# A graph network layer with routed experts: expert weights loaded in four chained parts, the input added under the last attention head, register reads moved

## The reference, cut to what matters

```python
x = x + relu(agg + res)                    # L0_gnn: 12 heads of 64, relu over all 768 columns
z = layernorm(x)
top = argmax(z @ Wg + bg)                  # L0_ffn: one of 4 experts for each node
h = gelu(z @ W1[top] + b1[top])            # 768 -> 384
x = x + h @ W2[top] + b2[top]              # 384 -> 768
# L1_gnn: dinv = rsqrt(degree), used from here on
```

## Time and profile before

| | us |
|---|---|
| median of 3 runs (lowest, highest) | 1097.67 (1097.63, 1098.87) |
| profiled execution, its time | 1098.94 |
| profiled execution, its span | 1097.2 |
| PE busy | 992.9 (90%) |
| DVE busy | 611.1 (56%) |
| ACT busy | 288.5 (26%) |
| POOL busy | 60.2 (5%) |

### The profile page before, as it was taken

How to read it: one execution, slowest core, us unless ns; L and a number is a source line. 1 busy time by engine, 2 the same in 40 slices (tenths; PEclk the granted TensorE clock), 3 DMA queues, 4 the chain that set the end, 5 groups by cost and what they waited for, 6 DMA issues and landing times. The chain is left out here.

```text
span 1097.2 us, 15664 instructions
## 1 busy us (share of the span) xinstructions
PE 992.9 (90%) x5694; PEld 801.6 (73%) x5694; DVE 611.1 (56%) x1273; ACT 288.5 (26%) x780; POOL 60.2 (5%) x114
## 2 busy tenths in 40 slices
PE   5999998999999999948099993999999999999996
PEld 4777675999999999935056662566998557878784
DVE  7787796999999999967223222753211112232331
ACT  1434342355444555113011100122111012200100
POOL 2000000000000000011112210100000000000000
PEclk9999999899999999969589997899999999999999
DMA  3100000000000000347412224324200001200001
GB/s 118 33 1 1 24 29 1 23 25 24 23 23 34 34 23 32 130 136 273 182 44 87 87 80 176 128 76 159 88 1 1 1 0 56 86 29 29 21 15 51
DMA packets 23912, 65.26 MB, mean 59 GB/s; under 512 B 4104, under 2 KB 7956, under 8 KB 23728
## 3 DMA queue, kind: packets, MB, share of 16 engines
q1 hardware_dynamic: 21408, 54.20, 13.6%
q0 software_dynamic: 2080, 10.23, 2.8%
q10 hardware_dynamic: 368, 0.07, 0.0%
HBM read 47.74 MB, written 16.76 MB: 59 GB/s over the span
## 5 line engine op out<-in xcount | busy, mean ns | idle before, releaser
L754 PE MATMUL O<-X,masks 125*125 125x264 f32 x1200 | 280.9, 333 | 2.8 <-DVE masks L891 2.8
L751 PE MATMUL O<-X,CSR 125*125 125x132 f32 x1080 | 245.6, 227 | 0.0
L754 PEld LDWEIGHTS O<-X,masks 125*125 125x125 f32 x1200 | 222.9, 188 | 3.0 <-issue 3.0
L891 DVE SCALAR_TENSOR_TENSOR masks<-a2b,NA,CSR 125x375 fp32r<-125x375 f32 (+1 forms) x360 | 212.9, 645 | 17.4 <-PEq L738 9.6
L751 PEld LDWEIGHTS O<-X,CSR 125*125 125x125 f32 x1080 | 205.6, 190 | 0.0
L389 PE MATMUL pc<-ohs_a,ohd 125*125 125x512 f16 (+1 forms) x399 | 84.1, 352 | 0.0
L1572 PE MATMUL pw<-W 128*125 128x384 f32 x240 | 81.5, 497 | 1.0 <-ACT W L1708 1.0
L1792 DVE SCALAR_TENSOR_TENSOR UL<-pw,dinv,UH 125x768 fp32r<-125x768 f32 x20 | 20.4, 1018 | 110.9 <-ACT UH L1715 110.9
L1572 PE MATMUL pw<-region,xr_or_h 128*125 128x384 f32 x240 | 77.6, 486 | 0.0
L581 DVE TENSOR_SCALAR ohs_a<-iota,srcf 125x1250 f16<-125x1250 f16 x132 | 71.4, 541 | 0.0
L578 DVE TENSOR_SCALAR ohd<-iota,dstf 125x125 f16<-125x125 f16 x220 | 53.8, 251 | 28.5 <-PE pc L389 25.3
(11 more groups left out here) (225 smaller groups left out, 1388.9 us busy)
## 6 DMA issues: line engine op xcount, KB each, us to landing
a2b<-a_rows SPq DMA_DIRECT2D x12, 610.4 KB
W<-in_L_ffn_W SPq DMA_DIRECT2D x1, 4608.0 KB, 15.9
WM<-in_L_ffn_W SPq DMA_DIRECT2D x1, 4608.0 KB, 27.6
xr_or_h<-in_x SPq DMA_DIRECT2D x10, 375.0 KB
region<-in_x SPq DMA_DIRECT2D x2, 1875.0 KB
z_rows<-region SPq DMA_DIRECT2D x10, 375.0 KB
region<-y_rows SPq DMA_DIRECT2D x10, 375.0 KB
x_rows<-xr_or_h SPq DMA_DIRECT2D x10, 375.0 KB
```

The lines of the kernel that those rows point to most:

```text
L751: nc.tensor.matmul(O[0:P, bank, d - d0, 2 * DP:4 * DP], CSR[:, s, d * P:(d + 1) * P], X[:, buf, s, 4:6, :].rearrange("p k d -> p (k d)"), ...
L754: ins = nc.tensor.matmul(O[0:P, bank, d - d0, 0:4 * DP], kept, X[:, buf, s, 0:4, :].rearrange("p k d -> p (k d)"), start=s == 0, stop=s == ...
L891: nc.vector.scalar_tensor_tensor(masks[:, s, 0:(d1 - d0) * P], a2b[:, buf, d0 * P:d1 * P], NA1[:, s, bass.ds(h, 1)], CSR[:, s, d0 * P:d1 * ...
```

## The change

Expert weights are loaded by expert, in four parts. The first is issued where all weights were; the second after the fifth store of z, once the first has landed; the third and fourth in the experts block, once the first three gathers have landed and each after the part before it. One semaphore counts them, and the first layer on PE waits for the part of its expert by the value in the register. The relu and the sum with the second copy of x leave `prepare`: eleven heads' columns are summed before `combine(H - 1)`, the last head's after it, each in two operations over five tiles. POOL answers two inverse roots, then makes constants, with two more answers between them; `gdeg` is asked and answered last, and `dinv` is made after `slot_out`. The turn of `b1` on PE and its copy on ACT go behind the tiles. PE reads its last two registers, and DVE its last nine, in the experts block. The slow path gets the same sum (it is not taken here).

```diff
--- before.py
+++ after.py
@@ -880,6 +880,14 @@
             def _(dve):
                 chains = [chain(dve, "dve_chain2"), chain(dve, "dve_chain2_slow")]
 
+                def add_x(k, heads):
+
+                    for n in range(2):
+                        h = slice(n * NT // 2, (n + 1) * NT // 2)
+                        c = slice(heads[0] * DH, heads[1] * DH)
+                        dve.wait_ge(s_xi[n], 16)
+                        k.mark(nc.vector.scalar_tensor_tensor(XR[:, h, c], XR[:, h, c], 0.0, XI[:, h, c], ALU.max, ALU.add))
...
                     head(H - 1, 1, last=True)
+                    k.wait()
+                    add_x(k, (0, H - 1))
                     for step in combine(H - 1):
                         pass
+                    k.wait()
+                    add_x(k, (H - 1, H))
+                    k.wait()
 
...
-        s_wm1, s_wm2, s_b4 = sem("moe_w1_in"), sem("moe_w2_in"), sem("moe_biases_in")
+        s_wm, s_b4 = sem("expert_weights_in"), sem("moe_biases_in")
+
+        def load_expert(sp, e):
+            sp.dma_start(WM1[:, e], a["L0_ffn_W1"][e].rearrange("(k p) h -> p k h", p=128)).then_inc(s_wm, 16)
+            sp.dma_start(WM2[:, e], a["L0_ffn_W2"][e].rearrange("(m p) d -> p m d", p=128)).then_inc(s_wm, 16)
+
...
-                    sp.dma_start(WM1, a["L0_ffn_W1"].rearrange("e (k p) h -> p e k h", p=128)).then_inc(s_wm1, 16)
-                    sp.dma_start(WM2, a["L0_ffn_W2"].rearrange("e (m p) d -> p e m d", p=128)).then_inc(s_wm2, 16)
+                    load_expert(sp, 0)
                     for t in range(NT):
                         sp.wait_ge(s_z3, t + 1)
                         sp.dma_start(z_t[:, t, :], ZA[:, t, :]).then_inc(s_zst, 16)
+                        if t == NT // 2 - 1:
+                            sp.wait_ge(s_wm, 32)
+                            load_expert(sp, 1)
                     sp.wait_ge(s_gt3, NT)
...
-                    answer_inverse_sqrt(pool, gdeg[:, :])
+                    answer_inverse_sqrt(pool, rstd[:, 0:1])
+                    answer_inverse_sqrt(pool, rstd[:, 1:2])
                     nc.gpsimd.memset(ones16[:, :], 1.0).then_inc(s_c3, 1)
                     nc.gpsimd.memset(minus1, -1.0).then_inc(s_c3, 1)
                     pool.wait_ge(s_c3, 2)
                     nc.gpsimd.affine_select(out=notabove[:, :], in_=minus1, compare_op=ALU.is_ge, fill=0.0,
                                             base=0, pattern=[[-1, P]], channel_multiplier=1).then_inc(s_c3, 1)
+                    answer_inverse_sqrt(pool, rstd[:, 2:3])
                     nc.gpsimd.iota(slot_i[:, :], [[1, 128]], base=-ST, channel_multiplier=0).then_inc(s_c3, 1)
                     nc.gpsimd.iota(tile_i[:, :], [[ST, 16]], base=0, channel_multiplier=0).then_inc(s_c3, 1)
                     nc.gpsimd.iota(node_i[:, :], [[P, NT]], base=1, channel_multiplier=1).then_inc(s_c3, 1)
+                    answer_inverse_sqrt(pool, rstd[:, 3:4])
                     nc.gpsimd.iota(spare_i[:, :], [[ST, 16]], base=N + 1, channel_multiplier=1).then_inc(s_c3, 1)
                     nc.gpsimd.memset(inner[:, :, 1:NT], 1.0)
                     nc.gpsimd.memset(inner[:, :, 0:1], 0.0).then_inc(s_c3, 1)
                     for e in range(NEXP):
                         ins = nc.gpsimd.memset(order[:, e:e + 1], float(NEXP - e))
                     ins.then_inc(s_c3, 1)
-                    for t in range(NT):
+                    for t in range(4, NT):
                         answer_inverse_sqrt(pool, rstd[:, t:t + 1])
+                    answer_inverse_sqrt(pool, gdeg[:, :])
                     pool.wait_ge(s_zst, 16 * (NT + 1))
...
-                    pe.wait_ge(s_b1, 16)
-                    nc.tensor.transpose(pb1[:, 0:NEXP * MH], b1r[:, :], ident[0:NEXP * MH, 0:NEXP * MH]).then_inc(s_b1t, 1)
+                    turn_z(0)
                     pe.wait_ge(s_wg, 32)
-                    turn_z(0)
...
                     turn_gates(NT - 1)
+                    pe.wait_ge(s_b1, 16)
+                    nc.tensor.transpose(pb1[:, 0:NEXP * MH], b1r[:, :], ident[0:NEXP * MH, 0:NEXP * MH]).then_inc(s_b1t, 1)
                     pe.wait_ge(s_oh3, 1)
...
-                    for j in range(NS):
+                    for j in range(NS - 2):
...
-                    act.wait_ge(s_b1t, 1)
-                    nc.scalar.copy(b1T[:, :, :].rearrange("p e m -> p (e m)"), pb1[:, 0:NEXP * MH])
...
-                    ch(nc.vector.tensor_scalar(gdeg[:, :], deg[:, :], 1.0, None, ALU.max),
-                       nc.vector.tensor_scalar(seen[:, :], deg[:, :], 0.0, None, ALU.is_gt))
-                    degrees = ask_inverse_sqrt(dve)
-
                     def prepare(t):
 
-                        if t % (NT // 2) == 0:
-                            dve.wait_ge(s_xi[2 * t // NT], 16)
-                        nc.vector.scalar_tensor_tensor(XR[:, t, :], XR[:, t, :], 0.0, XI[:, t, :], ALU.max,
-                                                       ALU.add).then_inc(s_x1, 1)
-                        dve.wait_ge(s_x1, t + 1)
...
+                    ch(nc.vector.tensor_scalar(gdeg[:, :], deg[:, :], 1.0, None, ALU.max),
+                       nc.vector.tensor_scalar(seen[:, :], deg[:, :], 0.0, None, ALU.is_gt))
+                    degrees = ask_inverse_sqrt(dve)
...
-                       nc.vector.memset(start[:, 0:1], 0.0),
-                       nc.vector.tensor_tensor(dinv[:, :], gdeg[:, :], seen[:, :], ALU.mult))
+                       nc.vector.memset(start[:, 0:1], 0.0))
...
-                    for j in range(NS):
+                    dve.wait_ge(s_ra, degrees)
+                    ch(nc.vector.tensor_tensor(dinv[:, :], gdeg[:, :], seen[:, :], ALU.mult))
+                    for j in range(NS - 9):
                         experts_dve.append(expert_of(dve, j))
...
+                    for j in range(SLOTS):
+                        sp.wait_ge(s_xs[j], 16)
+                    for e in range(2, NEXP):
+                        sp.wait_ge(s_wm, 32 * e)
+                        load_expert(sp, e)
                     sp.wait_ge(s_h, NS)
...
+                        pe.wait_ge(s_wm, experts[j] * 32 + 32)
...
                     turn_slots(0)
-                    pe.wait_ge(s_wm1, 16)
+                    for j in range(NS - 2, NS):
+                        experts_pe.append(expert_of(pe, j))
                     first_layer(0)
                     turn_slots(1)
-                    pe.wait_ge(s_wm2, 16)
...
                     copy_slots(0)
+                    for j in range(NS - 9, NS):
+                        experts_dve.append(expert_of(dve, j))
                     copy_hidden(0)
```

More of the change, by code:

```diff
@@ L1016, in slowly @@
                         k.end(H)
+                    k.wait()
+                    add_x(k, (0, H))
+                    k.wait()
                 either(dve, quickly, slowly)
@@ L1096, in program @@
             s_wg, s_b1, s_b1t, s_c3 = sem("gate_w_in"), sem("moe_b1_in"), sem("moe_b1_turned"), sem("constants3")
-            s_x1, s_z3, s_zt3 = sem("x1_done"), sem("z3_ready"), sem("z3_transposed")
+            s_z3, s_zt3 = sem("z3_ready"), sem("z3_transposed")
             s_ztc3, s_g3 = sem("z3t_copied"), sem("gates_done")
@@ L1216, in _ @@
                     copy_gates(NT - 1)
+                    act.wait_ge(s_b1t, 1)
+                    nc.scalar.copy(b1T[:, :, :].rearrange("p e m -> p (e m)"), pb1[:, 0:NEXP * MH])
                     act.wait_ge(s_eid, 1)
```

## The result

| | us |
|---|---|
| before, median of 4 runs (lowest, highest) | 1097.65 (1095.82, 1098.87) |
| changed kernel, median of 4 runs (lowest, highest) | 1087.38 (1086.01, 1087.85) |
| ratio, 95% interval | 0.9906 [0.9889, 0.9923] |
| changed kernel, profiled execution and its span | 1086.93, 1085.2 |

The change takes 10.3 us off; the forecast was 11.2 (1086.5). The page of the changed kernel (PE's busy tenths and its granted clock, 40 slices of 27.1 us) shows where: the three slices that read 4, 8, 0 in the earlier trace rows read 5, 9, 1.

The account below looks back on a forecast made before the run. The last store of z, delayed by weight loads on its five DMA engines, was taken to bound the gating block. -12.3 + 0.95 + 0.05 + 0.1 = -11.2 us, from 1097.67 to 1086.5, range 1085.0 to 1088.4 (chance 0.75).

Parts of the forecast that it names:

- What bounds the kernel: Gating block: PE waits for the first gather, which the last store of z releases; the slot map isn't the bound.
- Two parts fewer, -12.3: Gating block: two weight parts fewer ahead of the last store, 6.15 us each, bring it 12.3 us earlier.
- Block opens 0.95 later: Start of gating block: the last head's two operations and the waits delay all engines, +0.95 us.
- The sum under the last head, +0.05: Attention's end: two sums with x take 7.66 us in DVE's idle 7.64, costing +0.05 us.
- Compute chain: Gating block: first z near 484, L1265 at 512.8, map at 521.5, seven before the stores; no gain counted.
- Waits by expert and reads: Experts block: per-slot weight waits cost +0.1 us, up to 2 if exposed; moved register reads cost 0.
- Last store to first transpose, "plus 7.7": Barrier after gating: first transpose follows the last store's landing by 7.7 us, POOL's drain lying between.
- stores pass part 1: Rival, gating block: part 1 doesn't delay the last five stores, which end 6.15 us earlier; 1080.4 us, chance 0.04.
- What would show it: Signs in the trace: first z near 484, DMA share 0.32 with one bump, gather at 528 to 529, transpose 536.
- Gaps at the pieces: Rival, gating block: five DMA engines stand still around each part, stores end 4.6 us later; 1091.1 us, chance 0.09.
- a low clock in gating: Rival, gating block: PE's clock stays low, map at 531.9, later than the stores; 1089.8 us, chance 0.04.
- a dear register wait: Rival, `first_layer`: the register wait drains PE's sequencer, a cold start in each of 13 slots; 1103.7 us, chance 0.03.

Follow-up runs that it names:

- e4: Changed kernel with each store of z cut into 120 and 5 rows: 1081.03 us.
- e8: Kernel before, all weights still ahead of the stores, with each store of z cut into 120 and 5 rows: 1086.88 us.
- e2: Changed kernel with all expert weights loaded ahead of the stores as before, the rest of the change kept: 1098.34 us.
- e6: Changed kernel with a third weight part (part 2) also issued between the fifth and sixth store of z: 1093.05 us.
- e1: Kernel before with only the four weight parts, their chain and the wait by expert added: 1087.68 us.
- e7: Changed kernel with all thirteen register reads of PE and of DVE back in the gating block: 1085.85 us.
- e3: Changed kernel with part 1 of the weights issued behind the tenth store of z instead of the fifth: 1086.46 us.
- e5: Changed kernel with only the first gather in the gating block, the next two at the start of the experts block: 1084.43 us.
- e11: Changed kernel with z stores and y loads cut into 120 and 5 rows, one gather and four PE and ACT reads before the barrier: 1075.46 us.

## Why the prediction was right, point by point

**What bounds the kernel: right.** The gather waits for the last store in the changed kernel as in the earlier trace rows, with the map at 521.66, seven before it. e4 and e8 confirm it from the other side: with the stores out of the way the map releases the gather.

**Two parts fewer, -12.3: right in kind, 0.8 too much.** e2 against the changed kernel gives 11.5, e6 6.0 for one part; I had used 6.15 from the earlier trace rows, half the distance of two landings.

**Block opens 0.95 later: too little, it is 1.6 at SP's first issue.** From zero to SP's first issue are 480.20 - 479.09 = 1.11 us before and 480.73 - 478.05 = 2.68 after. The two operations take 0.89, near the forecast: two of 0.49 are 0.98, which leaves nothing of my 0.95 for the waits that it was to cover as well. What is missing is the wait that follows them: in the kernel before, DVE's sequencer is at its drain at 479.7, while L915 still runs; in the changed one the operations end at 479.80 and the drain starts at 480.4. At the gather e2 shows 1.3, so 0.3 more than forecast.

**The sum under the last head, +0.05: right.** Two operations from 466.56 take 7.55 in all (forecast 7.66), and L907 is then released by ACT's `ev` after 0.17 of idle time, where the earlier trace rows had 7.64. From the end of the last mask to the zero it is 11.40 us before and after.

**Compute chain: right.** L1285 (L1265 before) starts at 513.00 (forecast 512.8), `slot_out` at 521.66 (521.5), and first z is stored from 483.94 (484). With all weights ahead of the stores it gives nothing, as e2 shows. With two parts fewer it gives next to nothing either: the map alone would allow the gather at 521.66 + 0.80, 6.2 us before the stores do, and even e1's old chain is about even with its stores.

**Waits by expert and reads: right.** The slots take 8.73 us as before, and T to Y is 132.70 against 133.21. e7 shows no gain from the reads' new place.

**The sum.** To the gather -11.5 + 1.3 = -10.2, which is 60.82 - 50.63; the forecast to there was -11.3. G to T grew by 0.2, so -10.0 to T, and the medians differ by 10.3. The two errors, 0.8 and 0.3, have the same sign and are the 1.1 between the two. The two profiled executions differ by 12.0: beside the -10.0, the zero of before's was 1.04 later and T to the end 1.0 longer, and nothing ties these two to the change. One thing seems not to add up: e1's block opens at the old, earlier time, yet its gather is 50.57 from zero, like the changed kernel's 50.63. The map answers part of that: e1's gather stands where its map puts it (e8, released by the same map, has 50.62), so an earlier last store can't show there. How much earlier it was, the traces don't say for single stores. The biases, issued behind the last store, landed 53.6 us from zero in e1 (518.10 + 12.6) and 54.0 in the changed kernel (514.69 + 17.4), which is 0.4 and not 1.3; the rest stays open.

**Last store to first transpose, "plus 7.7": the right number for the wrong reason.** The prediction took POOL's drain for a fixed distance. It is three gathers, the last issued 2.75 us after the first and landed 4.7 after that. With the loads behind the stores it grew to 11.9 (e3), with one gather it fell to 4.7 (e5). In the changed kernel the queues are in the same state as before, so the number held. The rival "stores pass part 1", which was given 1080.4, would have missed its time by this: e3 makes its gather time (522.43 for 522.4) by another way, and gets 1086.46.

**What would show it: one sign wrong.** The share was to rise to about 1 once, between 496 and 503. For part 1 it rose twice (0.95 at 496 to 498, 0.33 at 500 to 502, 1.00 at 504 to 506 us), since SP's second issue of part 1 was held for 7.55 us (a full queue, I take it; that wasn't tested) and the other eleven engines got that piece only then. It rose a third time, to 1.00 from 518 to 522, for the biases, which the forecast of the share left out. Nothing seems to be lost by that: five engines of sixteen are a share of 0.31, and in steps of 1 us it never fell below 0.30 between 484 and 528, so no stretch shows the five at rest.

**The other rivals.** Gaps at the pieces, a low clock in gating and a dear register wait didn't come: G is at 528.68, the clock is 0.96 to 1.00 in the stretches from 492 to 510, in which the tiles are gated, and the slot cycle is the old one.

## What to carry to other kernels

When a chain ends in small stores behind large loads, look at the DMA share before moving the loads: 0.32 said that the stores used five engines of sixteen, and cutting 125 rows into 120 and 5 (e8) was worth as much as the reordering (10.3 us each), both together 16 us, and 20 to 22.5 with the next limits taken away. After each such step read all sequencers' drains at the barrier: the limit went from the stores to the map and the landed gathers, then to register reads that had been free. A load that is moved behind the critical stores comes to lie before the next transfers; part 1 moved there gained 6.1 us and lost 4.8 of them to slower gathers. When two edits give the same time, ask whether both stop at the same next limit: the parts alone (e1) equal the whole change, but stand even with the map and with DVE's register reads, so they have no room for a further step.

## What the hardware showed that was not expected

- POOL's drain at the end of a block lasts until the indirect DMAs issued before it have landed: 7.9, 11.9 and 4.7 us with three gathers, three gathers under load, one gather.
- A gather of 128 rows takes 4.1 to 5.0 us from issue to landing in the gating block of the other kernels and 9.3 to 9.5 in e3, behind 3840 KB that another queue had issued up to 519 us. The Trainium skill ("DMA: Bandwidth & Descriptors", section "Queues, rings and completion order") says that an engine takes turns between its queues by packet; no run here shows the turns, and if there are any, they didn't keep the gather from doubling.
- One DMA issue on SP can hold it for 7.55 us, where the same issue took 0.55 for part 0.
- The first layer right after the barrier takes 6.14 us in the changed kernel, after a stretch with a granted clock of 0.50 (1.2 GHz) and PE idle, and 5.7 to 7.2 in the others; later slots take 4.04 to 4.13. Nearly all of the spread of "T to Y" is that: without the first layer it is 126.4 to 126.8, e11 apart. Why the same layer takes up to 1.5 us more from one execution to the next stays open.
